# Convolution taps of a Mamba block added by accumulating DMAs instead of by GpSimd

## The reference, cut to what matters

```python
xz = einsum('bsd,ed->bse', xn, in_proj_w)            # xn: normalised, scaled and shifted x; 2 x 1024 columns
x_in, z = split(xz, 2, axis=-1)
u = silu(conv(x_in, conv_w, left padding 3) + conv_b)    # one filter of 4 taps for each of the 1024 channels
x_dbl = einsum('bsd,ed->bse', u, x_proj_w); dt_r, B, C = split(x_dbl, [64, 80], axis=-1)
dt = softplus(dt_r @ dt_proj_w.T + dt_proj_b);  A = -exp(A_log)
h[t] = h[t-1] * exp(dt[t] * A) + (dt[t] * u[t]) * B[t];  y[t] = sum over the 16 states of h[t] * C[t]
out = x + gate * (((y + u * D_param) * silu(z)) @ out_proj_w.T)
```

## Time and profile before

| | us |
|---|---|
| median of 2 runs | 2406.4 (2406.16 to 2406.65) |
| span of the profiled execution | 2405.4 |
| what lies around the span (median less span) | 1.0 |
| first scan to last scan's start (the 64 units) | 68.8 to 1910.5 |

### The profile page before, as it was taken

How to read it: one execution, slowest core, us unless ns; L and a number is a source line. 1 busy time by engine, 2 the same in 40 slices (tenths; PEclk the granted TensorE clock), 3 DMA queues, 4 the chain that set the end, 5 groups by cost and what they waited for, 6 DMA issues and landing times. The chain is left out here.

```text
span 2405.4 us, 24262 instructions
## 1 busy us (share of the span) xinstructions
PE 2232.3 (93%) x6966; PEld 1153.2 (48%) x6966; DVE 2163.1 (90%) x2363; ACT 1679.7 (70%) x3268; POOL 1908.1 (79%) x1244
## 2 busy tenths in 40 slices
PE   9899999989998999899989988998987999999999
PEld 3233434334433443344334333433333488988888
DVE  4899999999999999999999999999999966666666
ACT  3688777877787778778877887787555445466655
POOL 0699999999999999999999999999987822232225
PEclk9899999999999999999999999999998999999999
DMA  6610231041104110411051123103100121011113
GB/s 225 229 44 27 100 103 40 27 148 59 35 27 158 47 37 22 167 56 59 19 179 40 31 71 130 33 27 130 64 31 12 74 77 34 26 56 58 49 53 123
DMA packets 78050, 176.10 MB, mean 73 GB/s; under 512 B 7453, under 2 KB 10781, under 8 KB 77918
## 3 DMA queue, kind: packets, MB, share of 16 engines
q1 hardware_dynamic: 77918, 174.56, 21.6%
HBM read 157.23 MB, written 17.30 MB: 73 GB/s over the span
## 5 line engine op out<-in xcount | busy, mean ns | idle before, releaser
L1402 POOL TENSOR_TENSOR arena<-arena 128x1024 f32<-128x1024 f32 x512 | 1199.2, 2360 | 107.1 <-ACT arena L580 77.3
L1001 DVE TENSOR_TENSOR_SCAN arena<-ps,arena 128x512 f32<-128x512 f32 x1024 | 1241.7, 1256 | 1.3 <-ACT ps L580 1.2
L580 ACT ACTIVATE ps<-arena 128x512 f32<-128x512 f32 x1087 | 722.8, 681 | 367.2 <-DVE arena L1001 307.0
L318 PE MATMUL ps<-arena,keep 128*128 128x512 f32 x1782 | 863.3, 615 | 108.2 <-POOL arena L1402 74.9
L989 DVE TENSOR_TENSOR arena<-ps,arena 128x1024 f32<-128x1024 f32 x512 | 618.4, 1208 | 13.8 <-PE ps L318 11.1
L318 PEld LDWEIGHTS ps<-arena,keep 128*128 128x128 f32 x1782 | 333.6, 194 | 592.2 <-issue 338.4
L264 PE MATMUL ps<-arena 128*128 128x512 f32 x1024 | 459.9, 593 | 1.6 <-issue 0.8
L264 PEld LDWEIGHTS ps<-arena 128*128 128x128 f32 x1024 | 193.5, 190 | 248.8 <-issue 247.8
L580 ACT ACTIVATE arena<-arena 128x2 f32<-128x2 f32 (+2 forms) x599 | 228.4, 384 | 52.1 <-POOL arena L1347 17.1
L304 PE MATMUL ps<-arena 128*128 128x512 f32 x512 | 231.1, 592 | 0.0
L1359 POOL TENSOR_TENSOR arena<-arena 128x512 f32<-128x512 f32 x168 | 213.9, 1273 | 10.9 <-ACT arena L580 3.8
(11 more groups left out here) (146 smaller groups left out, 2701.7 us busy)
## 6 DMA issues: line engine op xcount, KB each, us to landing
arena<-scr_bc SPq DMA_DIRECT2D x128, 512.0 KB, 6.4
arena<-in_inT SPq DMA_DIRECT2D x128, 256.0 KB, 2.6
arena<-in_x SPq DMA_DIRECT2D x17, 512.0 KB, 4.3
scr_x<-arena SPq DMA_DIRECT2D x32, 256.0 KB, 2.2
arena_b<-scr_x SPq DMA_DIRECT2D x16, 512.0 KB, 3.8
arena_c<-scr_x SPq DMA_DIRECT2D x32, 256.0 KB, 2.9
out<-arena_c SPq DMA_DIRECT2D x32, 256.0 KB, 2.0
arena<-in_x SPq DMA_DIRECT2D x30, 256.0 KB, 3.3
```

The costliest lines, as they stand in the source:

```text
L318: last = e.matmul(YP, ident, hb[G % R][:, i, :], start=False, stop=(g == NG - 1 and i == n - 1))
L580: return e.activation(o_, i_, f, **kw)
L1001: e.tensor_tensor_scan(H, DA[s % 4], H, h0, MUL, ADD).then_inc(v_sc)
L1402: m_ = e.tensor_tensor(H, H, Ct[:, GN * g:GN * g + GN, :], MUL)
```

## The change

Three things change.

- `tap` no longer adds on GpSimd. GpSimd issues a DMA that reads `tp[:, w, :]` (128 x 512 float32, 256 KB) and adds it to u in SBUF. That a tap is done is now the DMA's semaphore, one of two that blocks use in turn (`tapped`). Before it issues the second or third tap of a block, GpSimd waits until the one before has landed; as before it also waits for ScalarE's copy.
- The three taps of a block stand 2, 4 and 6 slots behind its entry in `XMM`, no longer 2, 3 and 4. Two can now fall on one slot, so `TAP` holds lists.
- Block 5 moves from (5, 0) to (5, 3), block 7 from (6, 7) to (6, 4), and with them their evacuation and taps.

The semaphores of two late loads are shared with those of B and C (hence `D0`), which moves no work.

```diff
@@ -120,11 +120,11 @@
         d_C = [sem(f"d_C{g}") for g in range(NG)]
         d_xr = [sem(f"d_xr{i}") for i in range(2)]
         d_x1 = [sem(f"d_x1{i}") for i in range(2)]
-        d_rows = sem("d_rows")
+        d_rows, d_tap = sem("d_rows"), [sem(f"d_tap{i}") for i in range(2)]
+        tapped = lambda no, n: (d_tap[no % 2], 16 * (3 * (no // 2) + n))
         d_X = [sem(f"d_X{i}") for i in range(4)]
         d_M = [sem(f"d_M{i}") for i in range(2)]
-        d_xo = [sem(f"d_xo{i}") for i in range(4)]
-        d_out = [sem(f"d_out{i}") for i in range(4)]
+        d_xo, d_out, D0 = d_B[0:4], d_C[0:4], 16 * NCH
 
         p_cond, p_col, p_gb, p_tr, p_w, p_xp, p_dt, p_y, p_op = (sem("p_" + n) for n in
             ("cond", "col", "gb", "tr", "w", "xp", "dt", "y", "op"))
@@ -143,16 +143,19 @@
             sem("v_" + n) for n in ("wl", "lst", "lag", "lo", "k", "km", "q", "m8", "v", "rs", "rq", "mk", "df", "ks", "ac",
                                     "att", "y", "o"))
 
-        g_c, g_r1, g_r2, g_r3, g_rs, g_nm, g_tap, g_dt, g_du, g_gw, g_m, g_w = (sem("g_" + n) for n in ("c", "r1", "r2", "r3", "rs", "nm", "tap", "dt", "du", "gw", "m", "w"))
+        g_c, g_r1, g_r2, g_r3, g_rs, g_nm, g_dt, g_du, g_gw, g_m, g_w = (sem("g_" + n) for n in ("c", "r1", "r2", "r3", "rs", "nm", "dt", "du", "gw", "m", "w"))
         g_att, g_m1, g_mask, g_l1, g_l2, g_lrs, g_q, g_xo = (sem("g_" + n) for n in ("att", "m1", "mask", "l1", "l2", "lrs", "q", "xo"))
 
 
         after = lambda k, n: ((16 * k[0] + k[1] + n) // 16, (k[1] + n) % 16)
 
         AT = {"dt": 4, "soft": 7, "add": 6, "du": 7, "copy": 12, "yf": 6, "proj": (6, 14), "xdbl": (7, 3)}
-        XMM = {(3, 0): 0, (3, 4): 1, (4, 2): 2, (4, 8): 3, (4, 13): 4, (5, 0): 5, (5, 14): 6, (6, 7): 7}
+        XMM = {(3, 0): 0, (3, 4): 1, (4, 2): 2, (4, 8): 3, (4, 13): 4, (5, 3): 5, (5, 14): 6, (6, 4): 7}
         XEV = {after(k, 4): i for k, i in XMM.items()}
-        TAP = {after(k, (2, 3, 4)[w]): (i, 2 - w) for k, i in XMM.items() for w in range(3)}
+        TAP = {}
+        for k, i in XMM.items():
+            for w in range(3):
+                TAP.setdefault(after(k, (2, 4, 6)[w]), []).append((i, 2 - w))
         SILU = {(4, 3): (0, 2), (5, 9): (2, 5), (6, 15): (5, 8)}
 
         ZMM = {(1, 8): 1, (1, 10): 2, (3, 8): 1, (3, 11): 2, (5, 6): 1, (5, 10): 2, (7, 10): 1, (7, 13): 2}
@@ -644,7 +647,7 @@
                 for w in (2, 1, 0):
 
                     if no:
-                        e.wait_ge(g_tap, 3 * no - w)
+                        e.wait_ge(*tapped(no - 1, 3 - w))
                     k = 3 - w
                     act(tp[:, w, 0:k], old[:, w:3], ACT.Identity, scale=col("conv_w", 4 * i + w)).then_inc(a_xh)
                     act(tp[:, w, k:T], P[:, 0:T - k], ACT.Identity, scale=col("conv_w", 4 * i + w)).then_inc(a_tp)
@@ -656,7 +659,8 @@
                 if c == 0:
                     e.wait_ge(v_tap, 3 * hi)
                 else:
-                    e.wait_ge(g_tap, 24 * (c - 1) + 3 * hi)
+                    for i in (hi - 2, hi - 1):
+                        e.wait_ge(*tapped(8 * (c - 1) + i, 3))
                 v = u[c % 2][:, lo:hi, :]
                 act(v, v, ACT.Silu).then_inc(a_su)
 
@@ -1355,8 +1359,10 @@
                 v, no = u[c % 2][:, i, :], 8 * (c - 1) + i
                 e.wait_ge(a_tp, 3 * no + 3 - w)
                 if w < 2:
-                    e.wait_ge(g_tap, 3 * no + 2 - w)
-                e.tensor_tensor(v, v, tp[:, w, :], ADD).then_inc(g_tap)
+                    e.wait_ge(*tapped(no, 2 - w))
+                elif no >= 2:
+                    e.wait_ge(*tapped(no - 2, 3))
+                e.dma_start(v, tp[:, w, :], accum_op=ADD).then_inc(d_tap[no % 2], 16)
 
             def add(U):
                 e.wait_ge(a_ln, U + 1)
@@ -1386,7 +1392,8 @@
                 if U + 1 < NU and pr == AT["du"]:
                     du(U + 1)
                 if more and (j, pr) in TAP:
-                    tap(c + 1, *TAP[j, pr])
+                    for i, w in TAP[j, pr]:
+                        tap(c + 1, i, w)
                 if s % 2 == 1:
                     G = s // 2
                     g, H = G % NG, hb[G % R]
@@ -1422,7 +1429,7 @@
             def bias_rows(K):
                 for n in range(2):
                     i = xo_buf(K, n)
-                    e.wait_ge(d_xo[i], 16 * (K // 2 + 1))
+                    e.wait_ge(d_xo[i], D0 + 16 * (K // 2 + 1))
                     e.wait_ge(d_rows, 16)
                     e.tensor_tensor(o_bufs[i], o_bufs[i], rows[:, 2, :], ADD).then_inc(g_xo)
 
@@ -1593,7 +1600,8 @@
                     e.wait_ge(p_dt, NU)
                     e.wait_ge(p_w, len(WSEQ))
                     e.wait_ge(p_op, 32 * 7)
-                    e.wait_ge(g_tap, 24 * 7)
+                    for i in (54, 55):
+                        e.wait_ge(*tapped(i, 3))
                     e.wait_ge(g_gw, 8)
                     e.dma_start(x_bufs[0], x1v[0, 0]).then_inc(d_X[0], 16)
                     for h in range(2):
@@ -1632,7 +1640,7 @@
                 for n in range(2):
                     i, tile = xo_buf(K, n), 2 * k + n
                     if K >= 2:
-                        e.wait_ge(d_out[i], 16 * (K // 2))
+                        e.wait_ge(d_out[i], D0 + 16 * (K // 2))
                     else:
                         e.wait_ge(v_wl, 6)
                     e.dma_start(o_bufs[i], x1d[b, 128 * tile:128 * tile + 128, :]).then_inc(d_xo[i], 16)
@@ -1664,7 +1672,7 @@
                 store(K - 1)
             store(15)
             for i in range(4):
-                e.wait_ge(d_out[i], 16 * 8)
+                e.wait_ge(d_out[i], D0 + 16 * 8)
 
 
 PACK = [("c", 16), ("A_log", 128), ("ada_b", 8), ("ln_g", 4), ("ln_b", 4), ("conv_w", 32), ("conv_b", 8),
```

## The result

| | before | after |
|---|---|---|
| median, us | 2406.4 | 2475.5 (2474.03 to 2477.02, 2 runs) |
| ratio | | 1.029, 95% interval 1.026 to 1.032 |
| span of the profiled execution | 2405.4 | 2472.2 |

The changed kernel is slower by 69 us, 9.9 us for each of the 7 chunks with DMAs. The forecast was 2416 and the range ended at 2470. The direction is rival 1's, though the landing is shorter than that rival asked for.

A forecast was written before the change was run, and what follows sets the result against it. VectorE was taken as the bound; 1.9 + 0.5 - 1.1 = 1.3 to 1.5 us per chunk, times 7 chunks 10 us, on 2406.4 gave 2416 us. The forecast's own range was 2404 to 2440, the whole range 2392 to 2470.

The forecast's parts named there:

- rival 1: GpSimd is held by its own transfers, each tap waiting for the landing before: 2514 us, chance 0.22.
- VectorE is the bound, and at most its 25.2 us can come back: VectorE sets the pace; freeing GpSimd returns at most VectorE's 25.2 us of waits for TensorE, 1.0%.
- Issue 1.0 us: GpSimd's time to issue one tap DMA, taken as 1.0 us, near the 1.27 us addition it replaces.
- Landing 3.8 us: L, the time from a tap DMA's issue start until it has landed: 3.8 us, with ends 2.2 and 6.4.
- ScalarE at (3, 8), 1.9 us per chunk: Block 1's third copy waits for block 0's tap in the single `tp`, delaying `exps`; VectorE stalls 1.9 us per chunk.
- The other pairs of blocks are 5 or more slots apart ... and I count nothing there: Waits for `tp` between blocks other than 0 and 1: 1.7 us more room each, so no cost.
- nothing, at L = 3.8: Block 7's last tap at (6, 10), silu at (6, 15): 8.7 us, some 6 of it GpSimd's lag; no cost.
- What GpSimd wins back: From (3, 6) to (5, 6) GpSimd needs 59.1 us against 62.0, so it is 2.9 us less behind.
- the 1.1 us per chunk goes: VectorE's waits for TensorE in steady chunks, 1.1 us per chunk, vanish as GpSimd falls less behind.
- the prediction's formula: GpSimd's stretch (3, 6) to (5, 6) summed, each place the longer of landing and issue plus product: 59.1 us.
- about 8: GpSimd's lag behind VectorE at (5, 6) would be about 8 us, not 11.
- Block 5's move, 0.5 us per chunk: Block 5's evacuation at (5, 3) delays silu and z_mm's PSUM bank at (5, 6): 0.5 us per chunk, ends 0 and 0.9.

The follow-up runs named there:

- e7: The changed kernel with block 7's taps as plain copies to DRAM and the last silu not waiting for them: 2460.5 us.
- e3: The changed kernel with tap DMAs reading a constant tile, so ScalarE's copies do not wait for `tp`: 2443.2 us.
- e10: The changed kernel with DMAs accumulating into DRAM scratch; of the landing waits only GpSimd's for a block's tap before is left: 2480.7 us.
- e9: The changed kernel with DMAs accumulating a constant tile into DRAM scratch and no engine waiting for a landing: 2414.0 us.
- e8: The changed kernel with plain copies to DRAM scratch; of the landing waits only GpSimd's for a block's tap before is left: 2408.9 us.
- e14: The changed kernel with the DMA taps 2, 3 and 4 slots behind instead of 2, 4 and 6: 2565.6 us.
- e1: The kernel before with only blocks 5 and 7 moved, taps still GpSimd's additions 2, 3 and 4 slots behind: 2443.5 us.
- e5: The changed kernel with DMAs as plain copies of a constant tile to DRAM scratch and no engine waiting for a landing: 2400.8 us.
- m4: The kernel before with only the last tap of each of the 8 blocks as an accumulating DMA, spacing 2, 3, 4: 2421.9 us.
- m5: The kernel before with the last tap as an accumulating DMA for blocks 0, 2, 3, 5 and 6 only: 2398.4 us.
- e12: The changed kernel with DMAs accumulating the copies into DRAM; of the landing waits only ScalarE's for `tp` is left: 2449.0 us.

## Why the prediction was wrong

- *VectorE is the bound, and at most its 25.2 us can come back.* Right: scan and expand kept their durations, no run's median came under 2398, and all of the loss is VectorE's waits.
- *Issue 1.0 us.* Right: 0.85 to 0.88 us for most, 0.99 mean. The product's row behind an issue starts 0.6 us behind the issue's start, while the issue's row still runs, and lasts 2.65 instead of 2.36 us, so a place lasts 0.9 us longer, the length of the issue.
- *Landing 3.8 us.* A little high: 3.5 (the row of the changed kernel's page). For the chain the number came out by luck, since 0.5 us pass between a landing and GpSimd's next issue, which the prediction put at nothing: 4.0. The Trainium skill's figure, an estimate of 2.6 us from "DMA: Bandwidth & Descriptors", anatomy of one DMA, was too low for this form; plain copies of the same size, to DRAM, took 2.3 us.
- *ScalarE at (3, 8), 1.9 us per chunk.* Right: 2.00 us in the third chunk. (The "1.4 us of slack" is 1.97 by the rows, 638.50 to 640.47; the sum used the rows.)
- *"The other pairs of blocks are 5 or more slots apart ... and I count nothing there", and for block 7 "nothing, at L = 3.8".* Wrong. ScalarE's copies waited in 43 places, and the silu 7 times for 40.2 us in all. GpSimd was 10 us behind at (6, 10) and not 6, but the prediction's own numbers already asked for a wait: 8.7 less 6 leaves 2.7 us for a landing of 3.8. In the third chunk VectorE lost 3.19 us behind this silu. e7 puts 15 us on the silu of block 7 and e3 puts 32 on `tp`.
- *What GpSimd wins back, 59.1 us against 62.0 for the stretch from (3, 6) to (5, 6), and "the 1.1 us per chunk goes".* This is the step that failed. The sum took the longer of landing and issue plus product at each place, as if each product could start at once, put GpSimd's waits for ScalarE at nothing and its own landings at 2.2 us, and read a gain from the total. Measured in the third chunk: 655.46 to 721.80 us, 66.3, of which GpSimd waited 4.2 us for its landings and 7.2 for ScalarE, 4.5 of them for keep_state and 2.7 for a copy that had waited for the late TensorE. keep_state stands behind ScalarE's copies, which wait for GpSimd's landings: a loop of two engines and a DMA. I had looked only at what VectorE needs of ScalarE, the `exps`.
- *The total of a stretch as the price.* It is the same step, and it fails without the loop too. At e10's landing of 4.0 us the prediction's formula gives 60.0 us, less than 62.0, so no loss, and 62.5 with the 0.5 us behind each landing; e10 lost 67 us over e9. In the changed kernel GpSimd's lag at (5, 6) was 721.80 - 713.62 = 8.2 us, the "about 8" of the forecast, and this was luck: VectorE itself had taken 63.7 us for the stretch and not 57.65. TensorE had been late in between, and where the forecast took off 1.1 us, the third chunk had waits of 4.03 and 2.42 us for TensorE.
- *A late TensorE is just late.* It was assumed and never said. Behind idle times of 3.0 to 3.7 us its clock was at the lower level for 3.4 to 6.8 us: 3.13 and 1.55 us of the waits of 4.03 and 2.42 in the third chunk are, by an estimate from the matmuls' 6.73 and 5.15 against 3.60 us, this: 4.7 of the chunk's 11.8 us.
- *Rival 1, to decide only from L of some 5.2 us.* The mechanism was right and its threshold was wrong. The stretch was priced as an average; what counted was each distance of 3.48 us against each landing and the 0.5 us behind it. e8, e10 and e14 agree with this.
- *Block 5's move, 0.5 us per chunk.* The place showed 2.42 us. z_mm began 6.6 us behind y_fin (720.26 against 713.62), as forecast, but took 5.15 us and not 3.44 at the lower clock. Taken alone with the additions the two moves cost 36 us (e1), which the prediction had at 0.5 x 7.

How much of the loss is the clock cannot be told from these runs, since the clock was never held while a wait stayed. The time at the lower clock is not by itself the loss: e5 and e8 stood at the lower clock for 113 and 120 us and were within 2 us or under before. It counts where TensorE is already the one that VectorE waits for. Also open is which place makes m4 lose 14 us where m5 gains 9. The two differ in the last taps of blocks 1, 4 and 7, the last blocks of the three silus (the expectation of m4 named 2 and 5 by mistake). By the tables block 4's tap stands 3 slots ahead of block 5's evacuation and block 7's 4 slots ahead of its silu; no trace shows which it is.

## What to carry to other kernels

Replacing an instruction of an engine by a DMA that it issues gains little if the engine then waits for the landing: compare the landing, and the time until the waiter goes on, with the distance to the first waiter at each place, not the sums over a stretch, and follow what stands behind the waiting instruction to the engine that issues the DMAs, since a loop there hands the wait on. Of a chain of DMAs, the last link is the one to try first, block by block (m5 gained 9 us with five blocks, m4 lost 14 with all eight). And where the late engine is TensorE, price a gap of 3 us as the gap plus some matmuls at half the clock.

## What the runs showed of the hardware

- A 256 KB DMA that adds into SBUF, issued by GpSimd, landed in 3.5 us (median of 168, 3.2 to 5.5); a plain copy of the same size from SBUF to DRAM in 2.3 (e5, e8), one that adds in DRAM in 4.0 to 4.5 (e9, e10, e12). The mean issue was 0.99 us with accumulation in SBUF, 0.95 to 1.37 with accumulation in DRAM and 0.58 without.
- GpSimd's next issue began 0.53 us behind the landing that it waited for (median of 52 places), ScalarE's next copy 0.02 us behind.
- The product's row behind an accumulating issue lasted 2.65 us and overlapped the issue's row by 0.27; otherwise it lasted 2.36, and 2.37 behind the plain issues of e5. So it is not shown that the product itself is slower.
- TensorE's granted clock was 0.50 for some 6.8 us around and behind idle times of 3.04 and 3.66 us, and for some 3.4 us with one of 3.02 us.
